# Queries and keys turned by transposing DMA transfers instead of TensorE, in a kernel for attention and a mixture of experts

## The reference, cut to what matters

```python
def attn(x, ...):                       # x: (2, 2048, 256), 4 heads of 64
    xn = layernorm(x, ln_gamma, ln_beta)
    q, k, v = xn @ w_q.T, xn @ w_k.T, xn @ w_v.T        # split into heads
    qn = rmsnorm(q, q_gamma) * 64 ** -0.5
    kn = rmsnorm(k, k_gamma)
    return softmax(qn @ kn.T) @ v @ w_o.T + b_o
def ffn(x, gate_w, expert_w):           # 8 experts, the best one of each token
    return x + expert_w[argmax(x @ gate_w.T)] @ x
x = x + layernorm(attn(layernorm(x)))
x = x + layernorm(ffn(layernorm(x)))
```

## Time and profile before

| | |
|---|---|
| median of 3 runs | 691.83 us (691.82 to 695.93) |
| profiled execution | 692.4 us, of which its span, first to last instruction, is 690.5 us |
| TensorE's granted clock, mean | 0.967 of full speed |
| PE busy | 607.0 us, 88% of the span |
| DVE busy | 573.5 us, 83% |
| ACT busy | 534.2 us, 77% |
| POOL busy | 262.1 us, 38% |

### The profile page before, as it was taken

One profiled execution on the slowest core, in us unless ns is written; L12 is line 12 of the kernel. 1 busy time (PEld: TensorE's weight loads), 2 busy tenths in 40 slices (PEclk: granted clock), 3 DMA queues, 4 the chain that ended last, 5 costly groups with the idle time before them and its releaser, 6 DMA issues. The chain is left out here.

```text
span 690.5 us, 21513 instructions
## 1 busy us (share of the span) xinstructions
PE 607.0 (88%) x8717; PEld 424.9 (62%) x8717; DVE 573.5 (83%) x1115; ACT 534.2 (77%) x848; POOL 262.1 (38%) x422
## 2 busy tenths in 40 slices
PE   4899789999999999877898799999999997568880
PEld 2677446666666667755775366666666676446760
DVE  5999778998889889899987689887888898976762
ACT  4798878898889899765888798888888897445642
POOL 3344444333333332003677333333323320555563
PEclk9999999999999999999999999999999999979995
DMA  5941299889888996121222989898988963228120
GB/s 168 296 124 30 58 173 180 169 153 183 168 166 156 183 170 135 61 84 46 62 71 72 183 146 164 154 168 154 164 162 156 164 129 108 70 75 302 65 73 32
DMA packets 60664, 92.87 MB, mean 134 GB/s; under 512 B 7057, under 2 KB 29844, under 8 KB 60566
## 3 DMA queue, kind: packets, MB, share of 16 engines
q0 software_dynamic: 35088, 66.13, 49.9%
q1 hardware_dynamic: 24902, 25.37, 12.7%
q10 hardware_dynamic: 576, 0.00, 0.0%
HBM read 15.87 MB, written 14.66 MB: 44 GB/s over the span
## 5 line engine op out<-in xcount | busy, mean ns | idle before, releaser
L693 ACT ACTIVATE e_f<-banks,nbias,c_ 128x1024 f32<-128x1024 f32 x172 | 200.8, 1202 | 44.1 <-PE banks L1571 31.1
L1571 PE MATMUL banks<-qk_T 128*128 128x512 f16 (+1 forms) x1024 | 217.4, 384 | 12.2 <-ACT qk_T L631 4.8
L1615 PE MATMUL banks<-v_mm,e_l 128*128 128x65 f16 x2048 | 201.6, 193 | 0.0
L1615 PEld LDWEIGHTS banks<-v_mm,e_l 128*128 128x128 f16 x2048 | 185.9, 97 | 0.0
L1123 DVE TENSOR_TENSOR e_l<-e_f,e_h 128x1024 f16<-128x1024 f32 x100 | 120.3, 1224 | 22.1 <-DMA e_h<-e_f 16.4
L1613 PE MATMUL banks<-v_mm,e_h 128*128 128x65 f16 x1184 | 117.9, 194 | 1.9 <-DVE e_l L1123 1.3
L1614 PE MATMUL banks<-v_lo,e_h 128*128 128x64 f16 x1184 | 117.9, 192 | 0.0
L1613 PEld LDWEIGHTS banks<-v_mm,e_h 128*128 128x128 f16 x1184 | 108.0, 97 | 14.7 <-issue 2.6
L1571 PEld LDWEIGHTS banks<-qk_T 128*128 128x128 f16 (+1 forms) x1024 | 51.0, 96 | 103.6 <-issue 62.2
L1614 PEld LDWEIGHTS banks<-v_lo,e_h 128*128 128x128 f16 x1184 | 107.5, 99 | 9.6
L693 ACT ACTIVATE x_all<-banks,nbias,c_ 128x1024 f32<-128x1024 f32 x84 | 98.8, 1200 | 6.9 <-DVE e_l L1123 6.2
(11 more groups left out here) (294 smaller groups left out, 1250.6 us busy)
## 6 DMA issues: line engine op xcount, KB each, us to landing
e_h<-e_f POOLq DMA_DIRECT2D x86, 256.0 KB, 4.0
e_x<-e_f POOLq DMA_DIRECT2D x62, 256.0 KB, 3.8
e_h<-x_all POOLq DMA_DIRECT2D x42, 256.0 KB, 4.2
e_x<-x_all POOLq DMA_DIRECT2D x30, 256.0 KB, 4.6
x_all<-x SPq DMA_DIRECT2D x12, 512.0 KB, 4.3
rows_d<-e_x SPq DMA_DIRECT2D x1, 5180.0 KB, 24.5
qk_T<-rows_d SPq DMA_DIRECT2D x20, 259.0 KB, 6.1
qk_T<-qk_T SPq DMA_DIRECT2D x16, 256.0 KB, 4.8
```

The costliest lines, as they stand in the source:

```text
L693: act.activation(whole[s % ALL % NEF], ps_S[s % ALL % 3], ACT.Exp, bias=bias_of(h, k // NT), scale=CESC).then_inc(s_E, 1)
L1571: return pe.matmul(ps_S[s % ALL % 3][:, c * BANK:(c + 1) * BANK], k_T[rows, 1 - c if cross else c, h * N + j * P:h * N + (j + 1) * P], q_T ...
L1615: ins = pe.matmul(o, low[s % ALL % NLO][:, at], v[:, 0:DH + 1], start=False, stop=j == NT - 1, skip_group_check=True)
```

## The change

Instead of PE, DMA transfers that transpose on their way turn the rows, issued by SP. With that:
- `transpose_qk`, `move_qk`, `move_k` and `move_q` and their PSUM tiles go. That is 8 transposes on PE for each of 32 tiles, 28 copies at L631 and 4 at L636 on ACT, 4 copies at L1087 on DVE.
- `transposed_qk` on SP waits for the rows of tile n (`s_lo`) and issues two transfers, one for the four query blocks and one for the four key blocks, 128 KB each, straight into `qk_T`. Semaphores `s_tr`, one for each row buffer, tell of them.
- There are three row buffers instead of two. `high_qk` of tile n waits for the transfers of tile n - 3.
- The two transfers that swap the halves of a group's keys are issued between the first and the second tile of the next group, once the group's own transfers have landed.
- The first scores of a batch wait for the transfers of its first 8 tiles. POOL's rounding transfer of step 2 and DVE's subtractions of steps 2 and 3 wait until the last transfers out of the row buffers in their memory have landed.
- The filling of `rows_d` is issued by ACT's queue, at about the same time.
- `bias(0)` on DVE moves behind the sums of the batch's last tile.

```diff
-        qk_s = [a[:, 2048:2048 + 4 * H * DH].rearrange("p (h c) -> p h c", h=2 * H)
-                for a in (e_h16, e_l16)]
+        qk_rows = [a[:, at:at + 4 * H * DH] for a, at in ((e_h16, 2048), (e_l16, 2048), (e_l16, 3072))]
+        NROW = len(qk_rows)
...
-            sp.wait_ge(s_tid, TIDS)
-            sp.dma_start(rows_d.rearrange("(s p) w -> p s w", p=P).bitcast(u32), spread(absent[:, :], 1, NSL)).then_inc(s_init, 16)
...
+            def transposed_qk(n, at):
+                sp.wait_ge(s_lo, n + 1)
+                if n == 0:
+                    sp.wait_ge(s_wf, 2)
+                for i, plane in ((0, 0), (1, 1 + swapped(at))):
+                    sp.dma_start_transpose(qk_T[:, plane, :].rearrange("p (h n) -> p h n", h=H)[:, :, at * P:(at + 1) * P],
+                                           qk_rows[n % NROW][:, i * H * P:(i + 1) * H * P]).then_inc(s_tr[n % NROW], 16)
...
+            def queries_and_keys(b):
+                for at in range(NT):
+                    transposed_qk(b * NT + at, at)
+                    if at % TG == 0 and at:
+                        turned_keys(b, at // TG - 1)
+                turned_keys(b, NG - 1)
...
-                        pool.wait_ge(s_T2, b * NT + NT - 1)
+                        pool.wait_ge(s_tr[0], transposed(last_in(0, (b + 1) * NT)))
...
-                    qn, qs = qk_n[t % 2], qk_s[t % 2]
+                    qn, qs = qk_n[t % 2], qk_s[n % NROW]
                     act.wait_ge(s_qg, n + 1)
-                    if n - 1 > 0:
-                        act.wait_ge(s_T2, n - 1)
+                    if n >= NROW:
+                        act.wait_ge(s_tr[n % NROW], transposed(n - NROW))
...
+                    act.wait_ge(s_tid, TIDS)
+                    act.dma_start(rows_d.rearrange("(s p) w -> p s w", p=P).bitcast(u32), spread(absent[:, :], 1, NSL)).then_inc(s_init, 16)
...
                         sums(n, at, t)
+                        if last and t == TG - 1:
+                            bias(0)
...
-                        if last and t == 2:
-                            bias(0)
...
-                    if s == b * ALL + 2:
-                        dve.wait_ge(s_T2, end)
+                    if s - b * ALL in (2, 3):
+                        dve.wait_ge(s_tr[s - b * ALL - 1], transposed(last_in(s - b * ALL - 1, end)))
...
-                pe.wait_ge(s_ke, end - 2)
+                for i in range(NROW):
+                    pe.wait_ge(s_tr[i], transposed(last_in(i, b * NT + QT)))
```

More of the change, by code:

```diff
@@ L227, in build @@
         s_kc = [sem(f"s_kc{i}") for i in range(NG)]
+        s_tr = [sem(f"s_tr{i}") for i in range(NROW)]
         s_id, s_ones, s_wf, s_qg, s_q2 = sems("id ones wf qg q2")
@@ L281, in keys, with transposed, last_in @@
             return k_T[rows, a, :].rearrange("p (h n) -> p h n", h=H)[:, :, gi * TG * P:(gi + 1) * TG * P]
+        def transposed(n):
+            return 32 * (n // NROW + 1)
+        def last_in(i, end):
+            return max(n for n in range(end) if n % NROW == i)
         def groups(body):
@@ L660, in a_act @@
                             high_y(g + 1)
-                        if not (first and t < 2):
-                            move_qk(n - 2, at - 2)
                         if t == 0 and not last and n:
@@ L1521, in a_pe @@
                             largest_everywhere(0)
-                        if not (first and t < 1) and not (last and t == TG - 1):
-                            transpose_qk(n - 1, t - 1)
                 def largest_T(qb):
```

68 lines of the change are left out of this document (13 added, 55 removed).

## The result

The changed kernel takes 703.6 us, median of 7 runs (698.1 to 707.1), where the kernel before takes 693.3 us beside it (7 runs, 691.4 to 695.9): a ratio of 1.0127 [1.0094, 1.0161], 1.3% slower and not 1.2% faster. The profiled execution took 705.8 us, its span 704.0 us.

What follows compares the result with a forecast made beforehand. The prediction took PE to bound attention and DVE, the fullest engine, the projection stages. Gains of 6.2 and 2.8 us less 1.0 us at the start made 8.0 us, so 683.8 us by the median, range 678 to 715.

Steps and rivals of the forecast that it cites:

- What the transfers cost: Projection stages: transposing transfers overlap like plain ones, landing 0.7 + 4 to 5 us after their rows; 0 us.
- PE and ACT in the projection: Both projection stages: without transposes and copies, DVE's waits for ACT's squares go; 6.2 us gained, 0 to 9.2.
- The first exponential after the last squares: Entry to attention: earlier table load, later bias and dropped copies bring exponentials forward; 2.8 us gained, 0 to 4.5.
- The start: First tiles: the filling shares the DMA engines, so tile 0's pair may come late; 1 us lost, 0 to 5.
- late start: Rival, batch 0: filling delays weights and first tiles, ACT and DVE lose 4 to 5 us; 689 us; 16%.
- The swap transfers: Keys' swap copies on SP, one more tile's wait later, used at steps 4, 8 and 12 of attention; 0 us.
- The transfers set the pace: Rival, projection stages: a pair takes over 3.45 us and stretches both; 713 us at 4.2 us a pair; 22%.
- step 2 later than 11.6 us behind the first exponential: Sign of being wrong, at attention's start: DVE's subtraction of step 2 comes later than the 11.6 us of before.
- the forecast: Whole kernel: 679 to 688 us, from the gains grown to 9.2 and 3.6 or shrunk to 5 and 0; 62%.
- The two pages: Transposing transfers: one page's 1309 ns a block would mean 10.5 us a tile; the other says as fast as regular ones.

Runs made afterwards that it cites:

- the profile taken again: The changed kernel itself, word for word, run and profiled once more on another occasion: ratio 1.0089 to the kernel before, span 698.0 us.
- the run with the small parts: Kernel before with only the filling of the rows' memory in ScalarE's queue and the first bias behind tile 15's sums: ratio 0.9995.
- its four repairs: Changed kernel with first four roundings on ScalarE, third group's key copies later, eight unread matmuls at group boundaries and a fourth row buffer: ratio 0.9896, 685.0 us.

## Why the prediction was wrong, point by point

- **"What the transfers cost"**, 0 us in the sum: this step failed, and it turned the sign. For the quiet stretch it was right: an issue takes 1.27 us and not 0.72, but with 2.5 us to landing a pair is there some 4 us behind its rows, a little sooner than supposed. What it left out is the place where attention starts. There the last three pairs, a group's swap copies and the first roundings meet on one queue and the same 16 engines. In the profile taken again tile 15's rows were done at 82.5 us; its pair stood 2.6 us behind tile 14's, was issued in 3.5 and landed 2.0 later, at 90.6: 8.1 us, where the prediction had 0.7 + 4 to 5. The rows came 1.5 us later than supposed, too. From the first exponential to the thirteenth this cost 5.7 us in batch 0 and 3.9 in batch 1, 9.6 in all (in batch 1 the variants that leave this place alone lose 1.8 to 2.4). Moving four roundings to ScalarE gave everything back, by less traffic and by quicker roundings both.
- From 40 to 70 us the DMA engines' share rises from 0.16 to 0.59 (0.49 with plain transfers). That is 12.9 us of all 16 engines for the 16 such transfers issued there, 1.6 us a tile, where I had 0.95. The stage took as long as with plain transfers, 55.3 and 55.1 us from first to last squares of batch 0.

The two stretches in the profile page's terms, before and then the changed kernel again:

```profile
40.00:70.00 30.00, 28.26 (x206) 22.52 (x204) 27.63 (x64) 26.38 (x61) 14.78 (x18) 1.00 0.16 44
```
```profile
40.00:70.00 30.00, 24.81 (x138) 19.07 (x139) 28.11 (x65) 20.32 (x53) 13.83 (x16) 1.00 0.59 111
```

- **"PE and ACT in the projection"** (term 6.2 us): this step failed as well. First to last squares went from 54.85 to 55.32 in batch 0 (0.5 lost) and from 59.45 to 57.46 in batch 1 (2.0 won), 1.5 us in all. With the 2.4 us of the start, which are in there and have a term of their own, 3.9 are left: too large by 2.3. The term was "DVE's waits and no more", 2.6 + 3.6 us, and these waits did not go. In the changed kernel again, 24 to 78 us and then 327.5 to 379 (DVE's waits: total, times, longest), and behind them ACT's waits for PE from 24 to 78 us, before and again:

```profile
DVE ss L964 <- ACT e_f L611: 3.7, 3, 2.6
```
```profile
DVE ss L964 <- ACT e_f L611: 2.8, 3, 1.7
```
```profile
ACT e_f L593 <- PE banks L1427: 5.6, 8, 2.0
```
```profile
ACT e_f L611 <- PE banks L1422: 11.5, 9, 2.9
```

  They are 6.5 us in all, in six waits instead of eleven, each right behind a group boundary. In groups 3 and 4 of batch 0 a step inside a group now takes 2.5 to 3.4 us instead of 3.0 to 3.9, and over a boundary 4.5 to 4.9 instead of 3.7 to 4.0: there PE, freed of its transposes, waits for y's low part, ACT for PE, and DVE for ACT. PE's busy time from 20.3 to 78.4 us fell to 47.8 us, not to about 40. Taking work from DVE changes little, so the pace is set by a round that runs over several engines. Which one (two PSUM banks taken in turn from projection to normalisation is my candidate) was only argued.
- **The first exponential after the last squares** (term 2.8 us): right. From the last squares of a batch to its first exponential it was 5.11 and 4.86 us before (that exponential is in the earlier trace rows) and 3.44 and 3.45 in the profile taken again: 1.7 + 1.4 = 3.1 us. The later bias alone makes 1.0 + 0.8 of it, as the run with the small parts shows. That nothing of it would be lost again by step 2's transfer was wrong, see above.
- **The start** (term 1 us, 0 to 5): 2.4 to 2.8 us, inside the bounds. The rival "late start" was true beside the rest, by the shared engines and not by the issue: with the filling in ACT's queue SP issued both loads of weights in 1.5 us, where the first alone had taken 9.27, while the DMA engines were as full (share 1.11 from 16 to 40 us). In the changed kernel:

```profile
21.02 1.50 SPq L332 DMA_DIRECT2D x_all<-weT  x2
```

- **The swap transfers** (0 us): elsewhere they land in 3.2 to 4.2 us; where attention starts they need up to 9.9 us instead of up to 5.6, and their issue sits in front of tile 13's pair. Moving one group's copies took that away on SP and was worth less than can be told.
- **"The transfers set the pace"**, the rival I had on the slower side, didn't happen: a pair is issued in 2.5 us where the queue is free, under 3.45. The loss came by a third way, a collision at one place, which I had named among the signs (step 2 later than 11.6 us behind the first exponential: it was 15.4, and 15.3 again) and not priced. That the time is inside my range says nothing for the forecast: the range reached so far for this rival and the late start.
- **The two pages.** "VectorE: DVE Perf Modes" in the Trainium skill (The three transpose paths, and its rules for kernel authors) steers away from the crossbar where TensorE will do. The runs agree in direction, not in size: SP went through eight blocks in 2.5 us, and nothing like the 10.5 us a tile that I had estimated from the page was seen. "Advanced Engine Details and Errata" in the Trainium skill (X-Bar Transpose) has transposing and regular transfers alike. The landing in a quiet stretch agrees (2.5 and 2.3 us); the issue doesn't (1.27 and 0.64 us), nor does the crowded place (8.1 and 5.0 us behind the rows).
- A slip in the ranges: 691.8 less (9.2 + 3.6 - 1.0) is 680 us, not 679.

The sum in the profile taken again, against before: start of the first squares +1.1, projection -1.2 and -3.4 up to the first exponential, attention +5.7, +1.0, +3.9 and -0.2, last stage +0.65: 7.5 us, the difference of the spans 698.0 and 690.5. The first profile has 6 us more, mainly 4.0 in the last stage and 2.8 in batch 0's projection, where two boundaries were slow.

The first of these is not the change's: the first squares start between 20.3 and 21.7 us in kernels of both kinds, at 20.3 to 21.5 in the four that keep the filling in SP's queue.

What stays open: which round sets the pace of the projection stage, what the 1.0 us between exponentials 12 and 127 of batch 0 is, and what decides whether 1.8 us of idle time bring the lower clock.

## What to carry to other kernels

Before moving a copy to DMA, ask who else wants the DMA engines and the issuing queue in the next 10 us, not what the transfer costs in a quiet stretch: here the quiet stretch had room and the seam between two stages had none. A wait that ends last is where a cause shows; taking away the wait alone (other buffers) made it worse, taking the roundings off the DMA engines cured it. The change itself was worth having once that was done: 1.0% with its four repairs, where the kernel before gains 0.2% from the roundings. The other repairs were not tried there; it had no slow boundary for the unread matmuls to mend. An engine that idles because its work was taken away can also come back at a lower clock. And an engine that is relieved in a round over several engines idles at the next meeting point, so the gain is to be read from the round's step times, not from one engine's waits.

## What the hardware showed that I had not expected

- A transposing transfer of 128 KB inside SBUF takes 1.27 us to issue on SP, a plain one 0.64. A pair takes 2.50 us in the quiet stretch (plain 1.28), 3.5 where swap copies stand in front of it in the queue, and up to 6.5 beside the roundings and 8.1 beside the filling.
- The small packets are not the transposing's: under 512 B there were 7057 before, 41873 with the transposing transfers and 40847 with plain ones into the same places, 544 and 528 for each transfer.

```profile
DMA packets 94454, 101.23 MB, mean 149 GB/s; under 512 B 40847, under 2 KB 63637, under 8 KB 94358
```

- A long transfer holds up the issue of the next one in its own queue, 9.27 us here, and not in another: with the filling in ACT's queue two such loads took 1.5 us, with the engines as full.
- Two executions with the same 1.8 us of idle time on TensorE differ: 1.00 of the clock behind it in one, 0.50 in the other, where two matmuls take 1.05 us instead of 0.63 for some 3 us. It was so in 18 of 44 such places, and in none of 16 where unread matmuls filled the idle time.
- The same stage at the end takes 112 to 113 us on three chips and 124 to 126 on another, in each kernel alike.
